# Block attention: scores right behind the first head's turn, masks ahead of them, and the copies of turned probabilities elsewhere

## The chip, the cores and the metric

The kernel runs on one core of a Trainium2 chip. Its engines are PE (matmuls, with weight loads shown apart as PEld), DVE (vector), ACT (scalar), POOL (GpSimd) and SP (which issues DMAs). Each takes its own instructions in order, and semaphores tie them together. The metric is the device time of one execution in microseconds (us), the median of several.

## What is computed

The program is two transformer layers in one launch, on 4 x 256 tokens of width 256. The change lies in the attention of the second layer, which in the reference is (cut to what matters; there are 16 heads of 16 columns, and 8 blocks of 32 keys):

```python
gate = jnp.einsum('bshd,bnhd->bhsn', q, km)          # km: mean key of a block
gate = jnp.where(selfb, POS, jnp.where(future, NEG, gate))
vals, idx = jax.lax.top_k(gate, TOPK)                # 4 blocks for each query
mask = sel_tok & causal
scores = jnp.einsum('bihd,bjhd->bhij', q, k) * d ** (-0.5)
scores = jnp.where(mask, scores, NEG)
p = jax.nn.softmax(scores, axis=-1)
o = jnp.einsum('bhij,bjhd->bihd', p, v)
```

After it come a normalisation, the output projection and a feed-forward part with low-rank experts.

## The kernel before

The 4 x 16 pairs of batch and head are numbered n = 0 to 63 and handled in 16 rounds Q of four (QUADS = 16). Heads of a round use 32 rows of PE each, so their scores run side by side, each into a PSUM bank of its own (SCORE_BANK). The 256 queries of a head are two tiles of 128 on the partitions; with a causal mask the first needs 128 keys and the second 256, so a head's scores are 384 columns. PE takes each of these fp32 products in two passes, so a round has 16 score passes.

What happens to a head n, with the functions and the semaphores that tie them:

- PE, `scores1(Q)` (L2243) computes the scores of four heads, and then (L2249) adds the causal mask to the two diagonal tiles of each by a bf16 matmul with the identity; this raises `bl_s` once for each head. It waits for `bl_min`: all minima of round Q-1 must have been read out of the score banks.
- DVE, `masked_minimum(n)` (L1796) adds the bias of the chosen blocks, keeps the result in `masked` and takes the row minimum, in two instructions (128 and 256 columns); it raises `bl_min`.
- ACT, `exponents(n)` (L1214), two instructions, raises `bl_exp`.
- PE, `probs1_turn(n)` (L2259), called turn(n) below, transposes the three 128 x 128 tiles into bank 5 for an even n and bank 6 for an odd n, and raises `bl_t`. It waits until the copy out of that bank of the head two before is done: `bl_even` or `bl_odd`.
- ACT copies even heads out of bank 5, `even_probsT(n)` (L1220, `bl_even`), the DVE odd heads out of bank 6, `odd_probsT(n)` (L1805, `bl_odd`).
- PE, `values1(Q)` (L2270) multiplies by the values for the four heads, two rounds later; the DVE copies the result (`quad_out`, L1810), PE turns it back (`quad_turn`, L2278) and the DVE divides by the sum (`heads_out`, L1816, L1819).

Each engine's loop over Q is written out by hand, and its order is what the change edits. In the rounds 0 and 1 PE also does `shares` (eight transposes a round), and ACT makes the queries and biases of later groups (`own_queries` L1179, `own_bias` L1190). In round 16 PE runs `hidden1(0)` (L2315 and L2290), the first block of the feed-forward part, which waits for all minima and for POOL's split of its weights (`b13_split`, the last at L958). POOL works by itself through the stage: ranks of blocks, masks and splits of weights. When all scores are out, SP starts the loads of `a2`, `w2` and `b2`.

Of the kernel before, what the change touches and what calls it, by code (L numbers as in the profile page):

```python
# [18 lines left out]
P = 128  # L19
B, S, D = 4, 256, 256  # L20
TOK = B * S
NT = TOK // P
QT = S // P
# [48 lines left out]
QUADS = 2 * GROUPS  # L72
# [227 lines left out]
def program(nc, t, y):  # L300

    ctx = ExitStack()
    with ctx:
# [667 lines left out]
        def _(act):  # L971
# [245 lines left out]
            def even_probsT(n):  # L1217
                act.wait_ge(bl_t, n + 1)
                at_least(act, bl_v, n // 4 - 1)
                act.activation(probs1T[:, n % 8, :], bank[5][:, 0:3 * P], ACT.Copy).then_inc(bl_even, 1)  # L1220
# [18 lines left out]

            own_bias(1)  # L1240
            for Q in range(QUADS + 1):
                if 0 < Q <= QUADS:
                    even_probsT(4 * Q - 4)
                if Q == 1:
                    share_out(1)
                if 1 < Q < QUADS and Q // 2 + 1 < GROUPS:
                    own_queries(Q // 2 + 1, Q % 2)
                if 0 < Q <= QUADS:
                    even_probsT(4 * Q - 2)
                if Q < QUADS:  # L1250
                    exponents(4 * Q)
                    exponents(4 * Q + 1)
                if Q in (0, 1, 2):
                    share_out(Q + (Q > 0))
                if Q % 2 and 1 < Q // 2 + 1 < GROUPS:
                    own_bias(Q // 2 + 1)
                if Q == QUADS:
                    act.wait_ge(bl_s, GROUPS * HG)
                    act.wait_ge(w3_in, 32)
                    high_part("w13", 1)  # L1260
                    high_part("w13", 2)
                    act.wait_ge(bl_t, GROUPS * HG)
                    activated(0, 0)
                if Q < QUADS:
                    exponents(4 * Q + 2)
                    exponents(4 * Q + 3)
            act.wait_ge(bl_v, QUADS)

# [49 lines left out]
        def _(dve):  # L1318
# [159 lines left out]
            n = 11 + 2 * NT  # L1478
# [360 lines left out]
                                  ALU.subtract).then_inc(f_low, 1)  # L1839

            for Q in range(QUADS + 4):
                if Q > 3:
                    heads_out(Q - 4)
                if 2 < Q < QUADS + 3:
                    quad_out(Q - 3)
                if Q == QUADS + 2:
                    gated(0, 0)
                if 0 < Q <= QUADS:
                    odd_probsT(4 * Q - 3)
                if Q < QUADS:  # L1850
                    masked_minimum(4 * Q)
                    masked_minimum(4 * Q + 1)
                if 0 < Q <= QUADS:
                    odd_probsT(4 * Q - 1)
                if Q < QUADS:
                    masked_minimum(4 * Q + 2)
                    masked_minimum(4 * Q + 3)
                if Q == 0:
                    for d in (4, 5, 6, 7):
                        compare(dve, rest_heads, beats_rest, rest_beats, d)  # L1860
# [46 lines left out]
        def _(pe):  # L1907
# [324 lines left out]
                mm.then_inc(fill_mm, 1)  # L2232


            def scores1(Q):

                G, b, k, par, i = place_of(4 * Q)
                pe.wait_ge(bl_q, 2 * G + par + 1)
                at_least(pe, bl_min, 8 * Q)
                for q in range(QT):  # L2240
                    for n in range(4 * Q, 4 * Q + 4):
                        strip32 = slice(32 * (n % 4), 32 * (n % 4) + 32)
                        pe.matmul(bank[SCORE_BANK[n % 4]][:, q * P:(2 * q + 1) * P],  # L2243
                                  q_par[strip32, G % 2, par, q * P:(q + 1) * P],
                                  qkT[strip32, 2 + k, b * S:b * S + (q + 1) * P], start=(q == 0), stop=False,
                                  skip_group_check=True)
                for n in range(4 * Q, 4 * Q + 4):
                    diagonal = bank[SCORE_BANK[n % 4]][:, 0:4 * P].rearrange("p (q m) -> p q m", q=QT)[:, :, 0:P]
                    pe.matmul(diagonal, identb, along(tableb("causal"), (1, QT)), start=False, stop=True,  # L2249
                              skip_group_check=True).then_inc(bl_s, 1)  # L2250

            def probs1_turn(n):
                pe.wait_ge(bl_exp, 2 * n + 2)
# [137 lines left out]
            for Q in range(QUADS + 3):  # L2391
                if 0 < Q <= QUADS:
                    probs1_turn(4 * Q - 4)
                    probs1_turn(4 * Q - 3)
                if Q < QUADS:
                    scores1(Q)
                if Q == QUADS:
                    hidden1(0)
                if 0 < Q <= QUADS:
                    probs1_turn(4 * Q - 2)  # L2400
                    probs1_turn(4 * Q - 1)
                if Q < 2:
                    shares(2 * Q)
                    shares(2 * Q + 1)
                if 1 < Q < QUADS + 2:
                    if Q < 4:
                        pe.wait_ge(fill_out, len(fills()) + Q + 1)
                    values1(Q - 2)
                if Q > 2:
                    quad_turn(Q - 3)  # L2410
                if Q == QUADS + 1:
                    hidden1(1)
# [40 lines left out]
```

## Time and profile before

| | |
|---|---|
| median of 3 runs | 678.39 us (678.17 to 679.31) |
| profiled execution | 678.68 us |
| its span | 676.4 us |
| PE, PEld, DVE, ACT, POOL busy in the span | 653.9, 573.5, 498.3, 417.8, 298.4 us |
| granted clock of PE | 0.999 |

The span is what the profiler saw from the first to the last instruction; the time of the execution holds 2.3 us more around it. A busy engine need not be what sets the time: matmuls are pipelined and the ends that the profile shows for them are modelled. In the timeline a row is a run of like instructions, with its start, the time from the first one's start to the last one's end, and the idle time of the engine before it with what ended it.

### The profile page before, as it was taken

What the parts mean: (1) busy time and instruction counts of PE and PEld (TensorE: products, weight loads), DVE (VectorE), ACT (ScalarE), POOL (GpSimd) and SP (SyncE); (2) the same over time, 40 slices, a digit from 0 to 9 for tenths busy, and PEclk for the clock granted to TensorE, in tenths of its full rate; (3) what the DMA queues carried; (4) which work ended last, traced back from release to release, by engine and by line L of the source; (5) the groups of instructions that cost most, each with busy time, mean ns of one, the idle gap of its engine ahead of it and who ended that gap; (6) DMA issues with size and microseconds to landing.
All of it is one profiled execution on the core that took longest, in us unless ns stands there. A gap on an engine that the chain in (4) does not pass through costs nothing.

```text
span 676.4 us, 13824 instructions
## 1 busy us (share of the span) xinstructions
PE 653.9 (97%) x4756; PEld 573.5 (85%) x4756; DVE 498.3 (74%) x1422; ACT 417.8 (62%) x1084; POOL 298.4 (44%) x301
## 2 busy tenths in 40 slices
PE   5999999999999999999999998999999999999998
PEld 3777888898988989888888865566898999999997
DVE  7897867877778777877697798888677545655544
ACT  3866158888888878888865689998553322222221
POOL 1584155546464556452444318999525500400000
PEclk9999999999999999999999999999999999999999
DMA  8903034444535354343650000302100000000000
GB/s 316 379 2 102 1 117 141 149 139 149 183 103 174 108 172 128 114 134 115 227 239 1 1 1 1 111 1 85 43 1 1 2 17 1 1 16 1 2 16 16
DMA packets 26725, 59.43 MB, mean 88 GB/s; under 512 B 3146, under 2 KB 12748, under 8 KB 26272
## 3 DMA queue, kind: packets, MB, share of 16 engines
q1 hardware_dynamic: 23584, 50.35, 21.8%
q0 software_dynamic: 3072, 8.20, 3.6%
q8 instruction: 39, 0.64, 0.4%
q14 instruction: 30, 0.25, 0.1%
HBM read 48.24 MB, written 10.49 MB: 87 GB/s over the span
## 4 chain that ended last, share of the span: by engine, by line
PE 50%; ACT 5%; DVE 4%; issue 4%; POOL 3%; DMA 1%; POOLq 0%; ACTq 0%; DVEq 0%
PE bank L2290 10%; PE bank L2341 5%; PE bank L2315 5%; PE bank L2151 4%; ACT sb L1214 3%; PE bank L2357 3%; PE bank L1989 3%; PE bank L2198 3%; PE bank L2055 2%; PE bank L2075 2%; PE bank L2226 2%; PE bank L2066 1%; PE bank L1996 1%; PE bank L2046 1%; POOL sb L706 1%
## 5 line engine op out<-in xcount | busy, mean ns | idle before, releaser
L1073 ACT ACTIVATE sb<-bank,sb 128x256 f32<-128x256 f32 x128 | 59.6, 472 | 39.1 <-DVE sb L1578 34.7
L1281 ACT ACTIVATE h_parts<-sb 128x256 fp32r<-128x256 f32 x56 | 23.4, 418 | 76.4 <-DVE sb L1836 45.3
L2055 PE MATMUL bank<-sb 128*128 128x256 f32 x256 | 66.1, 381 | 0.0
L1578 DVE TENSOR_REDUCE sb<-bank 128x2 f32<-128x512 f32 x64 | 43.7, 683 | 27.6 <-PE bank L2055 26.4
L2290 PE MATMUL bank<-rounded,b_hi 128*128 128x256 f32 x224 | 63.0, 281 | 0.0
L2290 PE MATMUL bank<-rounded,b_lo 128*128 128x256 f32 x224 | 63.0, 281 | 0.0
L2290 PE MATMUL bank<-am_lo,b_hi 128*128 128x256 f32 x224 | 62.9, 281 | 0.0
L1827 DVE TENSOR_TENSOR sb<-sb,bank 128x256 f32<-128x256 f32 x56 | 23.5, 419 | 48.2 <-ACT sb L1238 48.2
L840 POOL DMA_INDIRECT expert_out<-sb x32 | 33.0, 1031 | 57.6 <-DVE sb L1520 43.9
L1080 ACT ACTIVATE sb<-sb 128x256 f32<-128x256 f32 x128 | 57.8, 505 | 0.1
L1238 ACT ACTIVATE sb<-bank 128x256 f32<-128x256 f32 x56 | 21.4, 381 | 54.3 <-PE bank L2290 54.3
L834 POOL DMA_INDIRECT sb<-rows_x,sb x32 | 32.8, 1024 | 41.7 <-PE bank L1989 20.0
L1989 PEld LDWEIGHTS bank<-sb 128*128 128x128 f32 (+1 forms) x384 | 46.1, 186 | 5.4 <-DVE sb L1514 3.3
L1589 DVE TENSOR_TENSOR pt_parts<-bank,pt_parts 128x512 fp32r<-128x512 f32 x64 | 43.7, 683 | 8.6 <-ACT pt_parts L1093 6.7
L1989 PE MATMUL bank<-sb 128*128 128x128 f32 (+1 forms) x384 | 49.2, 278 | 0.8 <-DVE sb L1514 0.8
L2055 PEld LDWEIGHTS bank<-sb 128*128 128x128 f32 x256 | 45.2, 190 | 4.8
L1838 DVE TENSOR_TENSOR h_parts<-sb,h_parts 128x256 fp32r<-128x256 f32 x56 | 27.0, 482 | 28.0 <-ACT h_parts L1281 28.0
L1214 ACT ACTIVATE sb<-sb 128x128 f32<-128x128 f32 (+1 forms) x128 | 46.7, 443 | 0.1
L2075 PE MATMUL bank<-pt_parts,xt_parts 128*128 128x256 f32 x256 | 46.0, 302 | 0.0
L2046 PE MATMUL bank<-rounded 128*128 128x512 f32 x160 | 42.7, 399 | 0.2 <-ACT sb L1102 0.2
L2290 PEld LDWEIGHTS bank<-rounded,b_lo 128*128 128x128 f32 x224 | 42.2, 188 | 0.0
L2290 PEld LDWEIGHTS bank<-rounded,b_hi 128*128 128x128 f32 x224 | 42.2, 188 | 0.0
(321 smaller groups left out, 1947.6 us busy)
## 6 DMA issues: line engine op xcount, KB each, us to landing
sb<-in_w_gate_up SPq DMA_DIRECT2D x32, 368.0 KB
sb<-in_w_down SPq DMA_DIRECT2D x32, 256.0 KB
sb<-in_w_pair SPq DMA_DIRECT2D x8, 704.0 KB
expert_out<-sb SPq DMA_DIRECT2D x1, 4096.0 KB, 22.4
sb<-expert_out SPq DMA_DIRECT2D x8, 512.0 KB, 7.0
sb<-in_w SPq DMA_DIRECT2D x1, 1792.0 KB, 12.8
sb<-in_b SPq DMA_DIRECT2D x1, 1792.0 KB, 7.4
sb<-in_sw_up SPq DMA_DIRECT2D x1, 1536.0 KB, 9.3
```

The lines of the kernel that those rows point to most:

```text
L1073: act.activation(probs[:, u % 4, q, :], bank[3 + u % 2][:, q * S:(q + 1) * S], ACT.Exp, scale=-1.0, bias=row_min[:, u % 4, q:q + 1], accum ...
L1080: ins = act.activation(probs[:, slot, q, :], probs[:, slot, q, :], ACT.Copy, scale=row_inv[:, slot, q:q + 1])
L1214: act.activation(probs1[:, n % 4, a:b], masked[:, n % 4, a:b], ACT.Exp, scale=-1.0, bias=row_min[:, n % 4, q:q + 1]).then_inc(bl_exp, 1)
L1578: dve.tensor_reduce(row_min[:, u % 4, :], bank[3 + u % 2][:, :].rearrange("p (q n) -> p q n", q=QT), AX.X, ALU.min).then_inc(at_min, 1)
L1589: dve.tensor_tensor(r(probs_lo[:, u % 2]), bank[5 + u % 2][:, :].rearrange("p (a b) -> p a b", a=QT), probs_hi[:, u % 2], ALU.subtract).th ...
L1989: mm = pe.matmul(bank[1][0:n, to:to + P], w_gu[s][:, k, a:a + n], xeT[s][:, k, :], start=(k == 0), stop=(k == KD - 1))
L2046: mm = pe.matmul(where[:, :], r(w[i][:, cols]), r(q[:, half]), start=(n == 0), stop=(n == len(terms) - 1))
L2055: mm = pe.matmul(bank[3 + u % 2][:, q * S:(q + 1) * S], qb[i][:, h, b * S + q * P:b * S + (q + 1) * P], keys[:, h, b * S:(b + 1) * S], sta ...
L2075: mm = pe.matmul(bank[2 + 5 * h][:, 0:S], r(v_parts[:, QT * b + k, :]), r(part[:, u % 2, k, :]), start=(n == 0), stop=(n == len(terms) - 1))
L2290: mm = pe.matmul(dst, lhs, rhs, start=False, stop=(n == len(terms) - 1), skip_group_check=True)
L2315: pe.matmul(dst, r(w[:, 2 * k + j, :]), r(x[:, k, :]), start=(i + j == 0), stop=False, skip_group_check=True)
L2341: mm = pe.matmul(bank[4 + k][:, h * CW:(h + 1) * CW], r(w[:, rows_]), r(x), start=(f + h + i == 0), stop=(f == NF1 - 1 and i == 2), skip_g ...
```

## The change

PE: the four causal masks of a round are a function of their own, `causal1(n)`, which starts each head's sum and waits only for that bank's minimum; they stand ahead of the scores, and the scores' second passes raise `bl_s`. In a round turn(4Q-4) comes first, then masks and scores, and then the other three turns; turn(4Q-3) stood ahead of the scores before. ACT: `even_probsT` of a round's first head moves from the start of the next round to between the exponents of the third and the fourth head; the other even copy goes behind the exponents of the next round's first head. DVE: the odd copies move back by two minima or more; that of head 4Q-3 now follows masked_minimum(4Q+1), and that of head 4Q-1 opens the next round.

```diff
--- before.py
+++ after.py
@@ -1239,16 +1239,15 @@
 
             own_bias(1)
             for Q in range(QUADS + 1):
-                if 0 < Q <= QUADS:
-                    even_probsT(4 * Q - 4)
                 if Q == 1:
                     share_out(1)
                 if 1 < Q < QUADS and Q // 2 + 1 < GROUPS:
                     own_queries(Q // 2 + 1, Q % 2)
-                if 0 < Q <= QUADS:
+                if Q < QUADS:
+                    exponents(4 * Q)
+                if Q:
                     even_probsT(4 * Q - 2)
                 if Q < QUADS:
-                    exponents(4 * Q)
                     exponents(4 * Q + 1)
                 if Q in (0, 1, 2):
                     share_out(Q + (Q > 0))
@@ -1263,6 +1262,7 @@
                     activated(0, 0)
                 if Q < QUADS:
                     exponents(4 * Q + 2)
+                    even_probsT(4 * Q)
                     exponents(4 * Q + 3)
             act.wait_ge(bl_v, QUADS)
 
@@ -1839,19 +1839,19 @@
                                   ALU.subtract).then_inc(f_low, 1)
 
             for Q in range(QUADS + 4):
+                if 1 < Q < QUADS + 2:
+                    odd_probsT(4 * Q - 5)
                 if Q > 3:
                     heads_out(Q - 4)
                 if 2 < Q < QUADS + 3:
                     quad_out(Q - 3)
                 if Q == QUADS + 2:
                     gated(0, 0)
-                if 0 < Q <= QUADS:
-                    odd_probsT(4 * Q - 3)
                 if Q < QUADS:
                     masked_minimum(4 * Q)
                     masked_minimum(4 * Q + 1)
                 if 0 < Q <= QUADS:
-                    odd_probsT(4 * Q - 1)
+                    odd_probsT(4 * Q - 3)
                 if Q < QUADS:
                     masked_minimum(4 * Q + 2)
                     masked_minimum(4 * Q + 3)
@@ -2232,22 +2232,24 @@
                 mm.then_inc(fill_mm, 1)
 
 
+            def causal1(n):
+                at_least(pe, bl_min, 2 * (n - 3))
+                diagonal = bank[SCORE_BANK[n % 4]][:, 0:4 * P].rearrange("p (q m) -> p q m", q=QT)[:, :, 0:P]
+                pe.matmul(diagonal, identb, along(tableb("causal"), (1, QT)), start=True, stop=False, skip_group_check=True)
+
             def scores1(Q):
 
                 G, b, k, par, i = place_of(4 * Q)
                 pe.wait_ge(bl_q, 2 * G + par + 1)
-                at_least(pe, bl_min, 8 * Q)
                 for q in range(QT):
                     for n in range(4 * Q, 4 * Q + 4):
                         strip32 = slice(32 * (n % 4), 32 * (n % 4) + 32)
-                        pe.matmul(bank[SCORE_BANK[n % 4]][:, q * P:(2 * q + 1) * P],
-                                  q_par[strip32, G % 2, par, q * P:(q + 1) * P],
-                                  qkT[strip32, 2 + k, b * S:b * S + (q + 1) * P], start=(q == 0), stop=False,
-                                  skip_group_check=True)
-                for n in range(4 * Q, 4 * Q + 4):
-                    diagonal = bank[SCORE_BANK[n % 4]][:, 0:4 * P].rearrange("p (q m) -> p q m", q=QT)[:, :, 0:P]
-                    pe.matmul(diagonal, identb, along(tableb("causal"), (1, QT)), start=False, stop=True,
-                              skip_group_check=True).then_inc(bl_s, 1)
+                        mm = pe.matmul(bank[SCORE_BANK[n % 4]][:, q * P:(2 * q + 1) * P],
+                                       q_par[strip32, G % 2, par, q * P:(q + 1) * P],
+                                       qkT[strip32, 2 + k, b * S:b * S + (q + 1) * P], start=False, stop=(q == 1),
+                                       skip_group_check=True)
+                        if q:
+                            mm.then_inc(bl_s, 1)
 
             def probs1_turn(n):
                 pe.wait_ge(bl_exp, 2 * n + 2)
@@ -2391,12 +2393,14 @@
             for Q in range(QUADS + 3):
                 if 0 < Q <= QUADS:
                     probs1_turn(4 * Q - 4)
-                    probs1_turn(4 * Q - 3)
                 if Q < QUADS:
+                    for n in range(4 * Q, 4 * Q + 4):
+                        causal1(n)
                     scores1(Q)
                 if Q == QUADS:
                     hidden1(0)
                 if 0 < Q <= QUADS:
+                    probs1_turn(4 * Q - 3)
                     probs1_turn(4 * Q - 2)
                     probs1_turn(4 * Q - 1)
                 if Q < 2:
```

Two places of the program as the engines get it. PE, one round in the middle of the stage, from the first turn of the round to the last (L2259 turns, L2243 scores, L2249 masks), before:

```order
L2259 MATMUL bank<-sb 128x128 [waits bl_even,bl_exp]
L2259 MATMUL bank<-sb 128x128 x2
L2259 MATMUL bank<-sb 128x128 [waits bl_odd,bl_exp]
L2259 MATMUL bank<-sb 128x128 x2
L2243 MATMUL bank<-sb 128x128 [waits bl_min,bl_q]
L2243 MATMUL bank<-sb 128x128 x3
L2243 MATMUL bank<-sb 128x256 x4
L2249 MATMUL bank<-cb 128x2x128 x4
L2259 MATMUL bank<-sb 128x128 [waits bl_even,bl_exp]
L2259 MATMUL bank<-sb 128x128 x2
L2259 MATMUL bank<-sb 128x128 [waits bl_odd,bl_exp]
L2259 MATMUL bank<-sb 128x128 x2
```

and after (L2261 turns, L2238 masks, L2247 scores):

```order
L2261 MATMUL bank<-sb 128x128 [waits bl_even,bl_exp]
L2261 MATMUL bank<-sb 128x128 x2
L2238 MATMUL bank<-cb 128x2x128 [waits bl_min] x4
L2247 MATMUL bank<-sb 128x128 [waits bl_q]
L2247 MATMUL bank<-sb 128x128 x3
L2247 MATMUL bank<-sb 128x256 x4
L2261 MATMUL bank<-sb 128x128 [waits bl_odd,bl_exp]
L2261 MATMUL bank<-sb 128x128 x2
L2261 MATMUL bank<-sb 128x128 [waits bl_even,bl_exp]
L2261 MATMUL bank<-sb 128x128 x2
L2261 MATMUL bank<-sb 128x128 [waits bl_odd,bl_exp]
L2261 MATMUL bank<-sb 128x128 x2
```

The turn that waits for `bl_odd` ahead of the scores has moved behind them, the masks have moved in front with waits for `bl_min`, and three turns now follow the scores.

The DVE, from a round's `quad_out` (L1810) on (L1805 the odd copy out of bank 6, L1796 the minima, four rows a head, with the score bank), before:

```order
L1810 COPY sb<-bank7 128x256 [waits bl_turn,bl_v]
L1805 COPY sb<-bank6 128x384 [waits bl_v,bl_t]
L1796 ISA sb<-bank3,sb 128x128 [waits bl_exp,bl_bias,bl_s]
L1796 ISA sb 128x1
L1796 ISA sb<-bank3,sb 128x256
L1796 ISA sb 128x1
L1796 ISA sb<-bank4,sb 128x128 [waits bl_exp,bl_bias,bl_s]
L1796 ISA sb 128x1
L1796 ISA sb<-bank4,sb 128x256
L1796 ISA sb 128x1
L1805 COPY sb<-bank6 128x384 [waits bl_v,bl_t]
```

and after:

```order
L1810 COPY sb<-bank7 128x256 [waits bl_turn,bl_v]
L1796 ISA sb<-bank3,sb 128x128 [waits bl_exp,bl_bias,bl_s]
L1796 ISA sb 128x1
L1796 ISA sb<-bank3,sb 128x256
L1796 ISA sb 128x1
L1796 ISA sb<-bank4,sb 128x128 [waits bl_exp,bl_bias,bl_s]
L1796 ISA sb 128x1
L1796 ISA sb<-bank4,sb 128x256
L1796 ISA sb 128x1
L1805 COPY sb<-bank6 128x384 [waits bl_v,bl_t]
L1796 ISA sb<-bank0,sb 128x128 [waits bl_exp,bl_bias,bl_s]
```

The copy that stood ahead of the minima of banks 3 and 4 is gone from there; the one behind them now is that of the round's first odd turn, and the second odd copy waits for the start of the next round.

## Rows read from the trace of the kernel before

**Rows 1.** the page: span, PE's busy time, granted clock in tenths

```profile
span 676.4 us, 13824 instructions
...
PE 653.9 (97%) x4756; PEld 573.5 (85%) x4756; DVE 498.3 (74%) x1422; ACT 417.8 (62%) x1084; POOL 298.4 (44%) x301
...
PEclk9999999999999999999999999999999999999999
```

**Rows 2.** timeline of PE: start and length in us, four places

```profile
399.35 0.94 PE L2243 MATMUL bank<-sb 32*128 32x128 f32 x16
...
413.05 0.94 PE L2243 MATMUL bank<-sb 32*128 32x128 f32 x16
...
467.16 0.94 PE L2243 MATMUL bank<-sb 32*128 32x128 f32 x16
...
471.31 0.48 PE L2315 MATMUL bank<-x_hi,w_hi 128*128 128x256 f32 x2
```

**Rows 3.** timeline of PE, rounds around 426: start, length, instructions

```profile
423.84 0.85 PE L2259 MATMUL bank<-sb 128*128 128x128 f32 x6
424.62 0.84 PE L2270 MATMUL bank<-sb 128*17 128x256 f32 x16
...
426.80 0.94 PE L2243 MATMUL bank<-sb 32*128 32x128 f32 x16
427.67 0.61 PE L2249 MATMUL bank<-cb 128*128 128x256 bf16 x4
428.46 0.84 PE L2259 MATMUL bank<-sb 128*128 128x128 f32 x6 [0.18 <-ACT sb L1220]
429.23 0.84 PE L2270 MATMUL bank<-sb 128*17 128x256 f32 x16
430.01 0.44 PE L2278 MATMUL bank<-sb 128*128 128x128 f32 x2
430.28 1.20 PE L2259 MATMUL bank<-sb 128*128 128x128 f32 x6
```

**Rows 4.** busy time by stretch of time: three windows

```profile
core 0: us, PE busy (x) PEld busy (x) DVE busy (x) ACT busy (x) POOL busy (x), PEclk, DMA share, GB/s
0.00:10.00 10.00, 2.92 (x10) 2.29 (x11) 5.54 (x24) 2.86 (x5) 1.78 (x7) 1.00 0.78 252
420.00:470.00 50.00, 47.56 (x570) 29.92 (x568) 45.03 (x235) 45.83 (x127) 48.85 (x40) 1.00 0.11 40
490.00:676.00 186.00, 180.94 (x1470) 178.20 (x1468) 104.76 (x208) 52.37 (x127) 35.00 (x35) 1.00 0.02 7
```

**Rows 5.** who waited for whom, 399 to 470: us, times, longest

```profile
PEld bank L2259 <- ACT sb L1214: 11.1, 27, 0.6
...
ACT sb L1220 <- PE bank L2259: 5.2, 15, 0.7
DVE sb L1796 <- PE bank L2249: 5.1, 14, 0.5
```

**Rows 6.** groups by line and form, 399 to 470: busy us, mean ns

```profile
L2243 PE MATMUL bank<-sb 32*128 32x256 f32 x128 | 9.8, 376 | 0.0
L2249 PE MATMUL bank<-cb 128*128 128x256 bf16 x64 | 9.8, 275 | 0.0
```

**Rows 7.** timeline of the DVE in the same round

```profile
427.99 0.29 DVE L1796 CUSTOM_DVE_ANT_1 sb<-bank,sb 128x128 f32<-128x128 f32 x1 [0.31 <-PE bank L2249]
...
428.55 0.08 DVE L1796 DVE_READ_ACCUMULATOR2_ANT sb<- 128x1 f32 x1
428.55 0.28 DVE L1796 CUSTOM_DVE_ANT_1 sb<-bank,sb 128x128 f32<-128x128 f32 x1
...
429.34 0.56 DVE L1805 COPY sb<-bank 128x384 f32<-128x384 f32 x1 [0.15 <-PE bank L2259]
```

**Rows 8.** timeline of ACT in the same round

```profile
427.84 0.47 ACT L1220 ACTIVATE sb<-bank 128x384 f32<-128x384 f32 x1
...
429.01 0.49 ACT L1220 ACTIVATE sb<-bank 128x384 f32<-128x384 f32 x1 [0.30 <-PE bank L2259]
```

**Rows 9.** timeline of POOL: low half of w13's first block

```profile
467.48 1.27 POOL L958 TENSOR_TENSOR w_lo<-sb,w_hi 128x512 fp32r<-128x512 f32 x1
```

## The prediction

> **What bounds the kernel now.** I read the page first: the span is 676.4 us, PE is busy for 97% of it and the granted clock stands at its upper level throughout [rows 1]. The change touches one stage, the block attention of the second layer, sixteen rounds of four heads. It begins with the first scores at 399.35 and hands over to the feed-forward part at 471.31, when PE starts hidden1(0) [rows 2]. From 426.80 to 467.16 there are nine rounds, 40.36 / 9 = 4.48 us each [rows 2, 3]. The stretches come next: in this stage PE is busy for 95%, the DVE 90%, ACT 92%, POOL 98% (on work of its own) [rows 4]. Nobody has slack to speak of, so the question is who waits for whom in a round. The waits of the stage say: PE's weight load waits 11.1 us for exponents, ACT's copy of turned probabilities 5.2 us for a turn (about 0.35 a round), the DVE's minimum 5.1 us for the masks [rows 5]. These are loops through three engines. What sets the new round is the longest loop after the change, so I lay it out link by link.
>
> **The change, part by part.** No instruction is added or removed: per round PE still has 16 score passes, 4 masks, 12 transposes, 16 value passes, 2 quad transposes; ACT and DVE have the same too. Three orders change.
>
> *Masks before scores, scores before turn(4Q-3).* From the start of the scores to the first minimum it is now 0.87 us of scores plus a mask of 0.28 plus a handover of 0.04, 1.19 in all [rows 3, 6, 7]. After the change the scores themselves release the DVE. All sixteen passes end 0.94 after the first starts [rows 3]; the first head's last pass is three places before the last, so I take 0.92, plus 0.04 = 0.96. The masks (4 at 0.11) and PE's change to the 32-row layout (below) come before, 0.54 us, but late in the round they find their bank free. By itself this looks like a gain: PE's scores no longer wait for exponents of a second head.
>
> *The odd copy.* Here is the price. Turned probabilities of odd heads go to one bank, bank 6. turn(4Q-1) on PE may write it only when the DVE has copied turn(4Q-3) out. Before, the DVE makes that copy ahead of the round's first minimum. After, it makes it behind masked_minimum(4Q) and (4Q+1), which wait for scores(Q). PE is in order, so behind turn(4Q-1) stand values1(Q-2), quad_turn(Q-3), the next turn(4Q), the next masks and scores(Q+1). That closes a loop:
>
> scores to first minimum 0.96; two heads' minima 2 x 0.56 = 1.12 (427.99 to 428.55) [rows 7]; the copy 0.55 [rows 7]; the handover to PE 0.15 (ACT's copy ends at 427.84 + 0.47 = 428.31, the turn that waited for it starts at 428.46; a DVE copy that PE waits for has no row) [rows 3, 8]; turn(4Q-1) and PE's change of layout 0.43 (an unhindered pair of turns takes 0.78 to the values; its six matmuls span 0.85 with the last at 0.27, so the step is 0.11 to 0.12, a turn 0.34 and the change 0.09) [rows 3]; values1 0.78 (429.23 to 430.01); quad_turn 0.27 (to 430.28); turn(4Q) 0.34; four masks 4 x 0.11 = 0.45 and the change 0.09 [rows 3, 6].
>
> Sum: 0.96 + 1.12 + 0.55 + 0.15 + 0.43 + 0.78 + 0.27 + 0.34 + 0.54 = 5.14 us, against 4.48 now: **0.66 us more a round**. Of it PE idles about 1.2 us in front of turn(4Q-1), where it hardly waits today.
>
> *The even copy* goes behind exponents(4Q+2). ACT then waits there for turn(4Q), and exponents(4Q+3) stands behind it. In a round of 5.14 this costs nothing more: ACT needs 4.48 - 0.35 = 4.13 [rows 5], so the odd loop covers it by 1 us. If that cover were gone it would bind at 4.13.
>
> *The whole stage.* Round 0 starts 0.54 later (masks ahead of the scores). Round 0 to 1 has no odd copy: 0.96, three minima at 0.56, a fourth with the read of its minimum 0.56 + 0.08 [rows 7], a handover 0.11, the last mask and the change 0.20, that is 3.59. Round 1 to 2 has eight share transposes (0.9) for the values and the quad turn with their change: 5.14 - 1.14 + 0.9 = 4.90. Round 2 to 3 has no quad turn: 4.87. So scores(3) starts at 399.35 + 0.54 + 3.59 + 4.90 + 4.87 = 413.25, against 413.05 now [rows 2], and twelve rounds of 5.14 lead to scores(15) at 474.9 against 467.16: **+7.8**. The last one leads to hidden1(0) after 5.14 - 0.54 = 4.60 (no masks), now 4.15: **+0.45**. Behind hidden1(0) now stand three turns instead of two, +0.34, and turn(63) must wait for the copy of turn(61): turn(61) to the start of its copy 0.53 (a pair starts at 428.46, its second turn 0.35 on, the copy at 429.34) [rows 3, 7], copy 0.55, handover 0.15, less two turns of 0.34, a wait of 0.55. Together **+0.9**.
>
> Everything later (values1(14) and (15), hidden1(1), the splits on ACT and POOL, the loads of a2 and w2 that SP starts once all scores are out) hangs on these and moves along. After 490 PE is busy for 97% [rows 4], and nothing there runs by a clock of its own, so nothing is given back. Sum +9.1 us: 678.68 of the profiled execution becomes 687.8. That execution lies 0.3 above the median of 678.39, so the forecast is 687.5.
>
> **Bounds of the unknown term.** The handover from scores to a minimum has no row. At the least, the first head's sum is there one step of the passes (0.21) after its last pass starts: 0.94 - 0.376 - 0.02 = 0.54 [rows 3, 6], so 0.75 + 0.04 = 0.79 instead of 0.96, 0.17 less in some 14 rounds: 685.1. At the most, four increments that now follow each other within 0.02 us are held apart as the masks' are, 0.11, and the first is late by that: 14 x 0.11 = 1.5 more, 689.0. I take the modelled end, since the modelled end of the mask lies 0.04 before the minimum that waited for it.
>
> **The rivals.**
>
> *Faster: the copy is in time.* If turn(4Q-1) did not wait, ACT's 4.13 would set the round: 14 x 0.35 = 4.9 us saved by scores(15). But hidden1(0) needs the split of w13 that POOL ends at 467.48 + 1.27 = 468.75 [rows 9], so it could start 2.5 earlier at the most; less the 0.9 of the tail this gives 1.6 off, 676.8. It decides from a loop under 4.48: 0.66 must be missing from the chain above, more than the spread of its one unknown link. The wait is in the code and each other link is a row. 4%.
>
> *The increments come late.* Before, four masks at 0.11 carry them; now four passes on concurrent 32-row strips. If the first were held back as bounded above, the time would be up to 689.0, more if all four preceded it. 8%. The Trainium skill (TensorE: Matmul & The Clock Gate, "The cost: per-tile semaphore tail") says that increments of concurrent tiles serialize at some 26 ns each. No row of this case has that, and by its figure the sum would be an estimated 0.4 us (one increment ahead of the minimum) to 1.5 us (all four) higher, 687.9 to 689.0.
>
> *The clock falls.* PE would idle 1.2 us in each round. At half clock some 3 us of PE links double: 14 x 3 = 42 us, about 730. Against it: in the first 10 us PE is busy for 2.92 and the granted clock is 1.00 [rows 4]. 1%. The Trainium skill (TensorE: Matmul & The Clock Gate, "The HAM clock gate (the 'warmup' mystery)") has the clock halved after idleness, which would give that outcome; by that stretch the trace does not show it here.
>
> *The loss is absorbed later.* The feed-forward part could turn out to wait for something that the stage doesn't delay, giving back some of the 9: 682 to 685. POOL's splits wait for ACT, which is late as well. 4%. That all of it is given back, so that there is no change: 1%.
>
> **How the numbers follow.** Forecast 82%, within 685.1 to 689.0 by its own bounds; late increments 8%, faster 4%, partly absorbed 4%, no change 1%, clock 1%. The range 685.0 to 689.3 takes in the forecast's bounds and the late increments and leaves out at most 2 in 10. About 0.2% (1.4 us) is what a measurement of this kernel can tell from no change. Slower 0.95, same 0.01, faster 0.04.
>
> **What the profile after would show.** PE: scores 5.1 us apart from the fourth round on; a wait of about 1.2 us before one turn in each round, released by the DVE's copy; no wait for the masks on the DVE. ACT: a wait before the copy behind the third head's exponents. hidden1(0) near 479.5, the feed-forward part as long as now. The forecast is wrong if turn(4Q-1) is not held, if the minimum starts at another point than 0.96 after the scores, or if the stage's end moves by another amount than the kernel's.

## The result, and the profile after

The changed kernel takes **688.45 us** (median of 4 runs, 688.34 to 689.08); the kernel before 678.43 (median of 4, 678.17 to 679.31). The ratio is 1.0139, 95% interval 1.0127 to 1.0151: 10 us slower. The forecast was 687.5, within 685.0 to 689.3. The profiled execution took 688.34, its span is 686.0.

The page answers to [rows 1]: PE does the same instructions in the same busy time, but its share is down from 97% to 95%, and the clock stays up.

```profile
span 686.0 us, 13808 instructions
...
PE 653.0 (95%) x4756; PEld 575.0 (84%) x4756; DVE 498.8 (73%) x1422; ACT 418.8 (61%) x1084; POOL 298.1 (43%) x301
...
PEclk9999999999999999999999999999999999999999
```

The waits of the stage, 399 to 478, answer to [rows 5] (engine, line <- whom it waited for: us, times, longest). PE's turn (L2261, was L2259) waits for the DVE's copy at L1805, fourteen times, a wait that the kernel before doesn't have. The DVE's wait for PE before a minimum is now for the scores themselves (L2247).

```profile
PEld bank L2261 <- ACT sb L1214: 22.3, 29, 1.2
PE bank L2261 <- DVE sb L1805: 14.4, 14, 1.0
...
DVE sb L1796 <- PE bank L2247: 11.9, 14, 1.6
ACT sb L1214 <- DVE sb L1796: 6.0, 14, 0.8
ACT sb L1220 <- PE bank L2261: 5.5, 12, 0.6
```

One round on PE's timeline (start, length; L2247 scores, L2261 turns, three matmuls each, L2272 values, L2280 quad turn, L2238 masks) answers to [rows 3]:

```profile
439.54 0.94 PE L2247 MATMUL bank<-sb 32*128 32x128 f32 x16
440.41 0.87 PE L2261 MATMUL bank<-sb 128*128 128x128 f32 x6
442.31 0.52 PE L2261 MATMUL bank<-sb 128*128 128x128 f32 x3 [1.03 <-DVE sb L1805]
442.76 0.85 PE L2272 MATMUL bank<-sb 128*17 128x256 f32 x16
443.53 0.44 PE L2280 MATMUL bank<-sb 128*128 128x128 f32 x2
443.81 0.49 PE L2261 MATMUL bank<-sb 128*128 128x128 f32 x3
444.14 0.60 PE L2238 MATMUL bank<-cb 128*128 128x256 bf16 x4
```

The same round on the DVE, which answers to [rows 7]:

```profile
440.50 0.29 DVE L1796 CUSTOM_DVE_ANT_1 sb<-bank,sb 128x128 f32<-128x128 f32 x1 [0.75 <-PE bank L2247]
...
441.61 0.55 DVE L1805 COPY sb<-bank 128x384 f32<-128x384 f32 x1
```

Read the two together as one loop: scores at 439.54, minimum at 440.50, the copy at 441.61 behind two heads' minima, the held turn at 442.31, values 442.76, quad turn 443.53, turn 443.81, masks 444.14, next scores 444.67. The profile calls 1.03 of the interval before the held turn idle; from where its six predecessors' steps end (440.41 + 0.68) it is 1.22.

At the end of the stage hidden1(0) (L2317) starts at 479.95 (was 471.31, [rows 2]), and behind it turn(63) waits for the copy of turn(61). The rows show turn(61) and turn(62), the held turn(63), then values1(14) and values1(15):

```profile
482.88 0.82 PE L2261 MATMUL bank<-sb 128*128 128x128 f32 x6
484.12 0.52 PE L2261 MATMUL bank<-sb 128*128 128x128 f32 x3 [0.42 <-DVE sb L1805]
484.56 0.84 PE L2272 MATMUL bank<-sb 128*17 128x256 f32 x16
...
486.50 0.84 PE L2272 MATMUL bank<-sb 128*17 128x256 f32 x16 [0.72 <-DVE sb L1819]
```

**Where the time went.** The executions differ ahead of the stage too, where the code is the same, so I measure the stage by itself, from the first scores to hidden1(1), the first work of PE behind values1(15) and the quad turn that follows it (that of round 14). Before: 399.35 to 477.89, 78.54 us. After: 400.56 to 487.47, 86.91, and 0.54 for the masks that now stand ahead of the first scores: 87.45. That is **8.91 more**. From hidden1(1) to the end of the span it is 198.51 before and 198.53 after. The rest of the 9.66 between the two profiled times is 0.67 ahead of the stage and some 0.1 around the span.

### The profile page after: what moved, and what is told of

The parts are those of the page before. It is cut to its first block, busy times and chain, and to the rows that moved or that the text cites. A ratio compares the mean times of both kernels' runs of the same rounds, so it can differ in the third digit from the quotient of the medians.

```text
span 686.0 us, 13808 instructions
## 1 busy us (share of the span) xinstructions
PE 653.0 (95%) x4756; PEld 575.0 (84%) x4756; DVE 498.8 (73%) x1422; ACT 418.8 (61%) x1084; POOL 298.1 (43%) x301
## 4 chain that ended last, share of the span: by engine, by line
PE 83%; DVE 12%; ACT 3%; issue 2%; DMA 0%; POOL 0%; DVEq 0%; ACTq 0%
PE bank L2292 10%; PE bank L2055 7%; PE bank L1989 7%; PE bank L2046 5%; PE bank L2343 5%; PE bank L2317 5%; PE bank L2075 4%; PE bank L2151 4%; PE bank L2066 4%; PE bank L1996 4%; PE bank L2359 3%; PE bank L2117 3%; PE bank L2198 3%; PE bank L2261 2%; PE bank L2247 2%
## 5 line engine op out<-in xcount | busy, mean ns | idle before, releaser
L1214 ACT ACTIVATE sb<-sb 128x128 f32<-128x128 f32 (+1 forms) x128 | 50.0, 446 | 6.0 <-DVE sb L1796 6.0
L1796 DVE CUSTOM_DVE_ANT_1 sb<-bank,sb 128x128 f32<-128x128 f32 (+1 forms) x128 | 37.9, 353 | 11.9 <-PE bank L2247 11.9
L2261 PE MATMUL bank<-sb 128*128 128x128 f32 x192 | 30.3, 280 | 16.0 <-DVE sb L1805 15.8
```

Of the source, the lines that this page charges most:

```text
L1214: act.activation(probs1[:, n % 4, a:b], masked[:, n % 4, a:b], ACT.Exp, scale=-1.0, bias=row_min[:, n % 4, q:q + 1]).then_inc(bl_exp, 1)
L1796: dve.tensor_tensor_reduce(masked[:, n % 4, a:b].rearrange("p (n c) -> p n c", c=CHUNK), bank[SCORE_BANK[n % 4]][:, a:b].rearrange("p (n c ...
L2261: mm = pe.transpose(bank[5 + n % 2][:, j * P:(j + 1) * P], probs1[:, n % 4, j * P:(j + 1) * P], ident)
```

## The experiments

"Round" is the mean from scores(3) to scores(15), an interval of twelve rounds. "Stage" is as above, with the 0.54 where the masks come first. In v1b_pool and v1a_pool the last quad turn (0.14) stands ahead of hidden1(1) too. Ratios are to the kernel before, run on the same chip; its median was 678.48 for the first four kernels, 679.32 for the next four, 679.08 for the three that follow and 678.73 for the last.

| kernel | median us | ratio, 95% interval | round | stage |
|---|---|---|---|---|
| before | 678.43 | 1 | 4.51 | 78.54 |
| after | 688.45 | 1.0139 [1.0127, 1.0151] | 5.13 | 87.45 |
| late_turn | 678.17 | 0.9998 [0.9989, 1.0007] | 4.09 | 78.53 |
| dve_back | 686.00 | 1.0106 [1.0090, 1.0121] | 4.96 | 85.85 |
| act_alone | 675.86 | 0.9959 [0.9945, 0.9973] | 4.28 | 76.11 |
| masks_alone | 678.67 | 1.0002 [0.9993, 1.0011] | 4.51 | 78.78 |
| dve_alone | 689.15 | 1.0144 [1.0128, 1.0159] | 5.25 | 88.87 |
| extra_in_loop | 696.06 | 1.0253 [1.0238, 1.0269] | 5.59 | 94.88 |
| extra_off_loop | 687.38 | 1.0123 [1.0107, 1.0138] | 5.13 | 87.45 |
| late_pool | 675.29 | 0.9940 [0.9927, 0.9954] | 4.09 | 74.55 |
| late_pool2 | 674.37 | 0.9934 [0.9922, 0.9946] | 4.09 | 73.43 |
| v1b_pool | 674.98 | 0.9936 [0.9923, 0.9948] | 4.11 | 74.63 |
| v1a_pool | 675.50 | 0.9952 [0.9939, 0.9964] | 4.11 | 75.00 |
| late_pool3 | 674.16 | 0.9934 [0.9920, 0.9947] | 4.09 | see there |

### late_turn: take what is queued behind the held turn out of the loop

```diff
                     probs1_turn(4 * Q - 3)
                     probs1_turn(4 * Q - 2)
-                    probs1_turn(4 * Q - 1)
...
                 if Q > 2:
                     quad_turn(Q - 3)
+                if 0 < Q <= QUADS:
+                    probs1_turn(4 * Q - 1)
```

> The changed kernel with one PE step moved: turn(4Q-1) stands behind values1(Q-2) and quad_turn(Q-3) instead of ahead of them. Everything else of the change stays. Theory A (turn(4Q-1), held by the DVE's copy of turn(4Q-3), carries the values and the quad turn behind it into the next round): the same chain without the values 0.78, the quad turn 0.27 and one change of layout 0.09 is 5.14 - 1.14 = 4.00 a round, so ACT's 4.13 binds: rounds of about 4.1, scores(15) about 5 earlier than in the kernel before. hidden1(0) then waits for POOL's split (468.75 in the profile before, against a start of 471.31 now), so 2.2 to 2.5 come out at the end: 676.2, in 675.5 to 677.5. Rival B (the masks ahead of the scores, or the scores' place, cost the 0.66 a round): the round stays near 5.1 and the time near 688. Rival D (the DVE's order alone, whatever PE does): it stays near 688 too.

The round falls from 5.13 to 4.09, as theory A has it and neither rival does: masks, scores, DVE and ACT are all as changed, and the loss in the rounds is gone. PE's round, with no wait in it:

```profile
436.37 0.94 PE L2247 MATMUL bank<-sb 32*128 32x128 f32 x16
437.24 0.87 PE L2261 MATMUL bank<-sb 128*128 128x128 f32 x6
438.04 0.84 PE L2272 MATMUL bank<-sb 128*17 128x256 f32 x16
438.81 0.44 PE L2280 MATMUL bank<-sb 128*128 128x128 f32 x2
439.14 0.85 PE L2261 MATMUL bank<-sb 128*128 128x128 f32 x6
439.82 0.62 PE L2238 MATMUL bank<-cb 128*128 128x256 bf16 x4
440.37 0.94 PE L2247 MATMUL bank<-sb 32*128 32x128 f32 x16
```

The time, however, is 678.17 and not 676.2. PE comes to hidden1(0) early and idles 4.08 us for POOL's split, which ends at 466.94 + 1.26 = 468.20:

```profile
466.94 1.26 POOL L958 TENSOR_TENSOR w_lo<-sb,w_hi 128x512 fp32r<-128x512 f32 x1
```

Then PE runs at half clock. The windows show that (PE, PEld, DVE, ACT, POOL busy, then the granted clock):

```profile
464.00:468.00 4.00, 0.22 (x3) 0.00 (x0) 1.54 (x6) 1.85 (x6) 3.84 (x5) 1.00 0.99 414
468.00:470.00 2.00, 1.70 (x8) 1.73 (x9) 0.00 (x0) 0.00 (x0) 2.00 (x4) 0.61 0.24 86
470.00:472.00 2.00, 2.00 (x11) 2.00 (x11) 0.00 (x0) 0.00 (x0) 1.79 (x2) 0.53 0.00 0
472.00:474.00 2.00, 2.00 (x26) 1.64 (x28) 0.56 (x1) 0.40 (x2) 0.00 (x0) 1.00 0.00 0
```

```profile
468.30 0.62 PE L2317 MATMUL bank<-x_hi,w_hi 128*128 128x256 f32 x2 [4.08 <-issue]
468.72 0.63 PE L2317 MATMUL bank<-x_lo,w_hi 128*128 128x256 f32 x2
...
472.75 0.27 PE L2261 MATMUL bank<-sb 128*128 128x128 f32 x1
```

The values 0.61 and 0.53 are means over two levels: in steps of half a microsecond the granted clock is 0.50 from 468.5 to 471.5 and 1.00 from 472.0 on. During the pause itself it is recorded as 1.00, so the rows don't tell when in it the clock fell.

hidden1(0) takes 4.45 us (468.30 to 472.75) instead of the 2.93 it takes in late_pool: 1.52 of the missing 2. late_pool tests that reading. The rest lies behind hidden1(0) and was left out of the expectation: from values1(14)'s quad turn to values1(15) it is 1.95 (474.27 to 476.22) against 1.15 before, 0.80 more, for a third turn and a longer wait for the DVE. Together 2.32, which is what the earlier start of hidden1(0) had gained; the stage is 78.53 against 78.54.

### dve_back: the DVE's order of before in the changed kernel

```diff
-                if 1 < Q < QUADS + 2:
-                    odd_probsT(4 * Q - 5)
...
+                if 0 < Q <= QUADS:
+                    odd_probsT(4 * Q - 3)
                 if Q < QUADS:
                     masked_minimum(4 * Q)
                     masked_minimum(4 * Q + 1)
                 if 0 < Q <= QUADS:
-                    odd_probsT(4 * Q - 3)
+                    odd_probsT(4 * Q - 1)
```

> The changed kernel with the DVE's order of before: the copy of turn(4Q-3) stands ahead of the round's first minimum, that of turn(4Q-1) between the second and the third. PE and ACT as changed. Theory A: one loop goes, but since PE makes turn(4Q-3) behind the scores, the minima now wait for that turn and its copy: scores to the turn 0.87, turn to its copy 0.53, copy 0.48, two minima 1.12, the other copy 0.48, two minima 1.20, handover to PE's last mask 0.10, mask and change of layout 0.20, in all 4.98 a round instead of 5.14. The time falls by 0.3 to 2 only: 687, in 686 to 688.5. Rival D (the DVE's order is the cause by itself): rounds of 4.5 and 678.5.

4.96 a round, where 4.98 was worked out. Rival D falls: with the DVE's order put back, the round stays 0.45 above the 4.51 of before. What is left comes from PE, which makes turn(4Q-3) behind the scores. With the copy ahead of the minima, the minima wait for that turn. The DVE's timeline shows it at the copy:

```profile
444.84 0.56 DVE L1805 COPY sb<-bank 128x384 f32<-128x384 f32 x1 [0.94 <-PE bank L2261]
445.32 0.28 DVE L1796 CUSTOM_DVE_ANT_1 sb<-bank,sb 128x128 f32<-128x128 f32 x1
```

### act_alone, masks_alone, dve_alone: one part of the change on the kernel before

act_alone takes over ACT's order alone (the lines of the diff above in the block of ACT), masks_alone `causal1` and the new `scores1` alone, dve_alone the DVE's order alone.

> The kernel before with ACT's new order alone (exponents(4Q) first, the even copy of turn(4Q-2) behind it, that of turn(4Q) between the exponents of the third and the fourth head). Theory A: ACT doesn't wait for a turn with nothing done, its loop of 4.48 loses some 0.2 to 0.3 a round; scores(15) is about 3 earlier, hidden1(0) is then held by POOL's split at 468.75, 2.5 earlier than now: 675.5, in 674.5 to 677. Rival C (ACT's copy behind the third head's exponents costs the time): slower than 678.4, up to 688 if it is the whole cause.

> The kernel before with the masks ahead of the scores alone (the scores release the DVE); turns, ACT and DVE as before. Theory A: the scores to the first minimum take 0.96 instead of 1.19 but the masks wait for the last minimum's bank and are 0.45 and a change of layout ahead of the scores; a round stays 4.5, the time 678.4 to 679.2. Rival B (masks first cost the 0.66 a round): 685 or more. A gain of 0.2 a round in the loop through the first minimum would give 675.5.

> The kernel before with the DVE's new order alone: the copy of turn(4Q-3) behind two minima, that of turn(4Q-1) at the start of the next round. Theory A: the loop of the forecast is closed here as well, with the masks behind the scores and two turns ahead of them: scores and mask to the first minimum 1.19, minima 1.12, copy 0.55, handover 0.15, turn(4Q-1) and change 0.43, values 0.78, quad turn 0.27, two turns 0.68, change 0.09: 5.26 a round, and about 9.7 at the end: 688.1, in 687 to 689.5. If the loss needed the masks or the scores moved (rivals B and D'): 678.5 to 680.

ACT's new order is a gain by itself: 0.41% faster, 4.28 a round. Rival C falls, and its sign was the opposite. The gain is cut short by POOL: hidden1(0) starts at 468.56, right behind the split (467.19 + 1.27 = 468.46).

```profile
467.19 1.27 POOL L958 TENSOR_TENSOR w_lo<-sb,w_hi 128x512 fp32r<-128x512 f32 x1
...
468.56 0.48 PE L2315 MATMUL bank<-x_hi,w_hi 128*128 128x256 f32 x2 [0.95 <-issue]
```

The masks make no difference that can be measured (1.0002, interval across 1). Rival B falls.

The DVE's order alone costs everything: 5.25 a round against 5.26 worked out. PE's timeline shows the same held turn, although nothing of PE was touched:

```profile
445.57 0.94 PE L2243 MATMUL bank<-sb 32*128 32x128 f32 x16
446.44 0.61 PE L2249 MATMUL bank<-cb 128*128 128x256 bf16 x4
446.89 0.49 PE L2259 MATMUL bank<-sb 128*128 128x128 f32 x3
448.58 0.52 PE L2259 MATMUL bank<-sb 128*128 128x128 f32 x3 [1.20 <-DVE sb L1805]
```

So the parts don't add up: -2.6, +0.2 and +9.8 us apart, +10.0 together with PE's turn order. They share one loop, and the longest loop decides. PE's turn order alone on the kernel before wasn't run.

### extra_in_loop, extra_off_loop: the same instruction in the loop and beside it

```diff
             def odd_probsT(n):
                 dve.wait_ge(bl_t, n + 1)
                 at_least(dve, bl_v, n // 4 - 1)
+                if n % 4 == 1:
+                    dve.tensor_reduce(bank[6][:, 3 * P:3 * P + 1], bank[6][:, 0:3 * P], AX.X, ALU.min)
```

extra_off_loop has `n % 4 == 3` there.

> The changed kernel with one more DVE instruction a round: a minimum over bank 6's 384 columns (its result is used by nobody) just ahead of the copy of turn(4Q-3), in the loop of the forecast. By the copy of as many columns (0.48 from one start to the next) it takes 0.4 to 0.5 us, d. Theory A: the round grows by the whole of d, 5.13 + d, and the time by 15 d (fourteen rounds and the wait of turn(63)): 688.45 + 6.0 to 7.5, about 695. If something else than this copy held the round: less than 2 us more.

> The changed kernel with the same additional DVE instruction, ahead of the copy of turn(4Q-1) at the start of the DVE's round, outside the loop of the forecast: the DVE waits there in any case for the scores (0.75 us before the first minimum). Theory A: no change of the round, 688.5 within 0.7. If the round were the DVE's own work in sum, it would cost as much as the one in the loop, 695.

In the loop the instruction takes 0.47 (from its start to the copy's):

```profile
444.67 0.56 DVE L1806 TENSOR_REDUCE bank<-bank 128x1 f32<-128x384 f32 x1
445.14 0.55 DVE L1807 COPY sb<-bank 128x384 f32<-128x384 f32 x1
```

The round is 5.59, 0.46 more; the stage is 7.43 longer, that is sixteen times 0.46 (one for each round with an odd copy) where I had said fifteen. The time of 696.06 is 1 above the 695 expected; the kernel before took 0.9 more on this chip, too. Off the loop, the same instruction at the start of the DVE's round costs nothing: 5.13, and a stage of 87.45, the same as the changed kernel's to 0.01. It only uses up waits of the DVE: that of 0.27 for the quad turn is gone, and that for the scores goes from 0.75 to 0.64:

```profile
442.26 0.56 DVE L1806 TENSOR_REDUCE bank<-bank 128x1 f32<-128x384 f32 x1
...
444.70 0.29 DVE L1796 CUSTOM_DVE_ANT_1 sb<-bank,sb 128x128 f32<-128x128 f32 x1 [0.64 <-PE bank L2249]
```

This shows the loop directly: what stands between the scores and that copy is paid in full in each round, the DVE's sum of work isn't paid. (The time of extra_off_loop is 1.1 us under the changed kernel's, more than the 0.7 allowed; its stage is not, its first scores come 0.92 earlier.)

### late_pool, late_pool2, late_pool3: where the gain of late_turn is held up

```diff
-            low_rank_parts(0)
+            low_rank_parts(0, (0,))
             pool.wait_ge(w3_in, 32)
...
+            low_rank_parts(0, (1,))
             low_rank_parts(1, (0,))
```

> late_turn with one more edit, on POOL: the split of the second low-rank factor of column group 0 stands behind the splits of x1 and w13 instead of ahead of them, so that w13's split ends 3.57 us earlier (two CASTs and two TENSOR_TENSORs on POOL from 461.29 to 464.86 in the profile before): near 465.2. Theory A, with what late_turn showed (PE idled 4.08 us before hidden1(0), then ran it at a granted clock near 0.53, 4.45 us instead of 2.92): PE now idles under 1 us there, the clock stays at 1.00, hidden1(0) starts near 465.4 and takes 2.9. The end comes 5 to 6 us earlier than in the kernel before: 672.8, in 672 to 674. If the clock falls there for another reason than the idleness, 1.5 more: 674.3. If hidden1(0) waits for something else than POOL, the time stays near 678.

late_pool2 moves one more:

```diff
-            low_rank_parts(1, (0,))
             for kind, n in weight_order:
+                if WT[kind, n] == 3:
+                    low_rank_parts(1, (0,))
```

> late_pool with one more move on POOL: the split of the first low-rank factor of column group 1 (3.7 us) stands behind the splits of w13's second and third block instead of ahead of them. In late_pool PE waited 0.75 us for the low part of w13's second block before hidden1(1), and POOL was busy without a gap until then; that wait goes, nothing else changes: 0.7 less than late_pool, 4.8 less than the kernel before, 673.9 on a chip where that one takes 678.7, in 673 to 675. If that factor is soon waited for, the 0.7 comes back later and the time is late_pool's.

late_pool: PE idles 0.61 before hidden1(0), for the last minimum and no longer for POOL, and the clock stays at 1.00:

```profile
466.64 0.47 PE L2318 MATMUL bank<-x_hi,w_hi 128*128 128x256 f32 x2 [0.61 <-DVE sb L1797]
...
475.01 0.50 PE L2318 MATMUL bank<-x_hi,w_hi_rest 128*128 128x256 f32 x2 [0.75 <-POOL w_lo L968]
```

The same hidden1(0) takes 2.93 us (466.64 to 469.57). So the half clock came with the idleness, and went with it. The time fell by 4.0 instead of 5 to 6. Within the stage hidden1(0) does start 5.78 earlier than before, but 1.79 is lost between it and hidden1(1): 1.0 ahead of hidden1(1), of which the profile calls 0.75 a wait for POOL (the last row), and the same 0.80 ahead of values1(15) as in late_turn, which the expectation had at nothing. late_pool2 removes that wait: its stage is 1.12 shorter. But from hidden1(1) to the end it takes 198.99 instead of 198.59, so 0.4 of it came back later; the time is 674.37, near the 673.9 expected.

> late_pool2 with hidden1(1) ahead of values1(15) on PE, and ACT's high parts of w13's second and third block ahead of its copy of turn(62). In late_pool2 PE waited 1.18 us before values1(15) for the DVE's division of heads, and ACT idled 2.66 before that copy. The 1.5 us of hidden1(1) now cover the wait; ACT's high parts are done near 467.7 and POOL's low part of the second block near 470.2, before PE comes to hidden1(1) near 470.5. So 1.2 less than late_pool2: 673.1 where the kernel before takes 679, in 672.5 to 674.5. If hidden1(1) then waits for POOL, or hidden1(3) for the last heads, the wait only moves, and the time is late_pool2's 674.4.

```diff
+                if Q == QUADS + 1:
+                    hidden1(1)
                 if 1 < Q < QUADS + 2:
...
                     values1(Q - 2)
```

The expected 1.2 didn't come. The wait of 1.18 before values1(15) is gone, and a wait of 0.96 has appeared before its quad turn, because hidden1(1) no longer stands between them:

```profile
474.16 0.84 PE L2275 MATMUL bank<-sb 128*17 128x256 f32 x16
474.94 0.44 PE L2283 MATMUL bank<-sb 128*128 128x128 f32 x2
476.33 0.44 PE L2283 MATMUL bank<-sb 128*128 128x128 f32 x2 [0.96 <-DVE sb L1813]
```

From the first scores to hidden1(2) it is 75.96 in late_pool2 and 75.89 here. The wait only moved.

### v1b_pool, v1a_pool: an order of its own

PE's loop against that of the kernel before (ACT and the DVE as the expectation says, POOL as in late_pool2; v1a_pool has `Q == QUADS` for hidden1(0)):

```diff
+                if Q < QUADS:
+                    scores1(Q)
                 if 0 < Q <= QUADS:
                     probs1_turn(4 * Q - 4)
-                    probs1_turn(4 * Q - 3)
-                if Q < QUADS:
-                    scores1(Q)
-                if Q == QUADS:
-                    hidden1(0)
-                if 0 < Q <= QUADS:
-                    probs1_turn(4 * Q - 2)
-                    probs1_turn(4 * Q - 1)
...
+                if 0 < Q <= QUADS:
+                    probs1_turn(4 * Q - 3)
...
                 if Q > 2:
                     quad_turn(Q - 3)
+                if 0 < Q <= QUADS:
+                    probs1_turn(4 * Q - 2)
+                    probs1_turn(4 * Q - 1)
                 if Q == QUADS + 1:
-                    hidden1(1)
+                    hidden1(0)
+            hidden1(1)
```

> A version of its own that keeps the masks behind the scores. PE's round: scores(Q) and masks, turn(4Q-4), turn(4Q-3), values1(Q-2), quad_turn(Q-3), turn(4Q-2), turn(4Q-1), so that each turn stands far behind the copy that frees its bank. DVE: three minima, the copy of turn(4Q-3), the fourth minimum, the heads' end of round Q-3, the copy of turn(4Q-1), the quad of round Q-2. ACT: exponents of two heads, the copy of turn(4Q-2), exponents of two, the copy of turn(4Q). hidden1(0) stands behind values1(15), and POOL's two splits are moved as in late_pool2. No loop is left that is longer than ACT's own work, 4.1 a round; hidden1(0) has nothing to wait for, neither have the turns and values behind the last scores. Stage 6.9 shorter than now: 671.8 where the kernel before takes 678.7, in 671 to 673. If moving values1(15) ahead of hidden1(0) leaves PE waiting for its copies, 1 to 2 more.

> v1b_pool with hidden1(0) a round earlier, ahead of values1(15): it covers the wait for the last turns' copies, but must wait for POOL's split if the rounds run ahead of it. Stage 6.5 shorter than now: 672.2 where the kernel before takes 678.7, in 671 to 673.5.

Both are faster than before, neither by as much as expected (some 3 us less) nor beyond late_pool2. The rounds are 4.11 as expected. Against late_pool2, the first scores to scores(15) take 0.62 more and from there to hidden1(1) 0.58 more (462.47 to 474.55 against 461.31 to 472.81). Of the 6.9 that v1b_pool was to save in the stage it saves 3.91: 0.50 up to scores(3) and 4.76 in the next twelve rounds, but from scores(15) to hidden1(1) it takes 12.08 where the kernel before takes 10.73. Two more turns stand there than before, and PE waits 0.20, 0.22 and 0.70 us for copies, where the expectation had it wait for nothing. How much each of these carries wasn't tried.

The fastest kernels found are late_pool2 and late_pool3, 0.66% faster than the kernel before and 2.0% faster than the changed one (674.37 / 688.45 = 0.980, from different chips). They keep the change and add one moved turn and POOL's moved splits. ACT's new order and POOL's splits without the rest of the change weren't run together, so how much of this gain needs the masks and the DVE's order is open.

## Why the prediction was right

- **The loop.** Every link was measured as it was summed: scores to first minimum 0.96 (0.96), two heads' minima 1.11 (1.12), copy and handover 0.70 (0.55 + 0.15), turn and change of layout 0.45 (0.43), values 0.77 (0.78), quad turn 0.28 (0.27), turn 0.33 (0.34), masks and change 0.53 (0.54). In all 5.13 against 5.14. The 0.66 a round came out as 0.62, since twelve rounds before take 4.51 each and not the 4.48 of the nine that were read; the forecast itself went by the starts of scores(3) and scores(15), not by the 4.48. That it is a loop and no chance likeness is shown by both extra instructions and by late_turn.
- **The unknown term**, the handover from the scores, came out at the modelled end, in the middle of its bounds. The rival of late increments had it up to 0.11 later. By the Trainium skill (TensorE: Matmul & The Clock Gate, "The cost: per-tile semaphore tail") the increments ahead would have cost 26 ns each; the row 439.54 to 440.50 is accounted for without any of them.
- **The stage.** First scores to scores(3) 13.34 (forecast 13.36), twelve rounds 61.53 (61.68), scores(15) to hidden1(0) 4.52 (4.60), from there to values1(15) 6.55 against 5.61 before, 0.94 more (0.9). Sum 8.9 (9.1).
- **Nothing given back.** From hidden1(1) on, 198.53 against 198.51.
- **ACT's copy.** Its wait behind the third head's exponents is there (ACT L1220, 12 times, 5.5 us) and costs nothing, as said. What the prediction didn't say is that ACT's new order alone is worth 2.6 us on the kernel before.
- **The rival "faster".** Its mechanism was sound: with the turn off the loop the round is 4.09 (4.13 was said), and POOL's split does cap it. Its price was a saving of 1.6 (676.8). That left out that the clock falls after the long pause there, which costs 1.52; late_turn measured 678.17 where the kernel before takes 678.48.
- **The clock.** 1.2 us of idleness a round left the granted clock at 1.00 throughout, as assumed; 4.08 us in one piece didn't. The row that the prediction set against this rival, a granted clock of 1.00 in the first 10 us, doesn't carry it: PE's instructions there take twice their time (last section). So that pauses of 1.2 us would do nothing was an assumption without a row to bear it, and that it came true is luck. The Trainium skill (same page, "The HAM clock gate (the 'warmup' mystery)") has the clock throttled unless activity releases it; late_turn agrees (0.50 behind the pause), the changed kernel's 1.2 us pauses don't show it.
- **The median** is 1.0 above the forecast although the stage was 0.2 under it: 0.67 is time ahead of the stage, which varies by itself (below), some 0.1 lies around the span and behind the stage, and 0.4 is where the two profiled executions lie against their medians (0.3 above before, 0.1 below after). The first and the last of these are chance of single executions; the forecast had reckoned with 0.3 of it only.

## What to carry to other kernels

When an instruction moves, don't ask whether its own engine has time, but which loop through several engines it joins: here a copy of 0.55 us that went behind two minima on the DVE closed a loop with everything queued behind a waiting turn on PE, and cost 0.62 a round. Write the loop as a sum of start-to-start distances; an instruction beside it is free and one in it costs its full length. The remedy can be on the other engine: put the instruction that must wait behind the work that needn't.

And once a loop is shortened, look for what it ran into next (here POOL's splits), in case the gain turns into one long pause of PE, after which its clock is halved.

## What the runs showed of the hardware

- **A pause can cost more than itself.** After 4.08 us without work the granted clock was 0.50, that is 1.2 GHz, from 468.5 to 471.5 in late_turn, and then 1.00 again: 1.52 us for hidden1(0). Pauses of 1.0 to 1.2 us, fourteen in a row with PE busy between them, brought nothing of the kind.
- **Increments from four concurrent 32-row strips** didn't hold back the first reader: 0.96 from the first pass to the minimum, the modelled end of that head's last pass (0.92) and 0.04, the same handover as from a single mask.
- **Time ahead of the stage varies.** With the 0.54 of the masks taken off, the first scores come at 398.66 (late_turn) to 400.46 (late_pool) in executions whose code is the same up to there. For differences of 1 us, compare the stage and not the end.
- **The granted clock of the first microseconds can't be read from the windows.** Part of that difference arises at the start of the program, in PE's first matmuls. Before and after, each with the same instructions (eight transposes, eight matmuls of 417 columns, eight transposes):

```profile
7.08 1.94 PE L1914 MATMUL bank<-sb 128*128 128x128 f32 x8 [7.08 <-DVE sb L1340]
8.95 3.59 PE L1929 MATMUL bank<-sb 128*128 128x417 f32 x8
12.38 1.04 PE L1914 MATMUL bank<-sb 128*128 128x128 f32 x8
```

```profile
8.73 5.00 PE L1929 MATMUL bank<-sb 128*128 128x417 f32 x8
13.57 1.04 PE L1914 MATMUL bank<-sb 128*128 128x128 f32 x8
```

The first eight transposes take 1.94, the next eight 1.04. The matmuls of 417 columns start 0.70 apart at first and 0.35 apart later; the change comes at about 10.2 us before and at about 12.8 after. This is the same factor of two as at the half clock of late_turn (steps of 0.21 instead of 0.12), and it follows 7 us in which PE had no work, yet the windows give 1.00 there. It isn't the DMA, which is busy for 97 to 100% of the time from 12 to 14 us before, with the short steps, as well. At 24 us the execution after is 1.19 behind the one before, at the first scores 0.67; what made up the other 0.52 wasn't looked into. Nor is it all of the difference: late_turn has its second eight transposes at 12.79 and yet the earliest first scores of all.
